# Prologue of a two-layer transformer kernel: split rests in a buffer of their own, the key sums on GpSimd behind the splits, the bias add between the first two quads

## The reference

```python
qkv = x @ W_attn + b_attn                     # 16 heads of 8 numbers each
q, k, v = heads(qkv)
s = einsum('bhtd,bhsd->bhts', q, k)
s = s - s.mean(axis=-1, keepdims=True)        # over all 1024 keys, later ones too
mad = abs(s).mean(axis=-1, keepdims=True) + 1e-06
s = s / mad * score_gain
s = where(causal, s, -1000.0)
r = maximum(s, 0.0) ** 4
att = r / (r.sum(axis=-1, keepdims=True) + 1e-06)
y = (att @ v) @ W_proj + b_proj
x = layernorm(x + y)
```

## Time and profile before

| what | value |
|---|---|
| median of the runs | 1172.78 us (1169.59, 1172.78, 1176.74) |
| the profiled execution, its own time | 1178.61 us |
| its span | 1176.9 us |
| TensorE, VectorE, ScalarE, GpSimd busy | 84%, 63%, 47%, 30% of the span |
| mean granted TensorE clock | 0.875 of full speed |
| prologue, to the first score matmul | 43.3 us |
| end of the first attention's quads | about 390 us |

### The profile page before, as it was taken

One profiled execution on the slowest core, in us unless ns is written; L12 is line 12 of the kernel. 1 busy time (PEld: TensorE's weight loads), 2 busy tenths in 40 slices (PEclk: granted clock), 3 DMA queues, 4 the chain that ended last, 5 costly groups with the idle time before them and its releaser, 6 DMA issues.

```text
span 1176.9 us, 18267 instructions
## 1 busy us (share of the span) xinstructions
PE 987.0 (84%) x6011; PEld 479.5 (41%) x6011; DVE 746.4 (63%) x1543; ACT 556.4 (47%) x607; POOL 351.6 (30%) x785
## 2 busy tenths in 40 slices
PE   5699999999999675398745788999999887999996
PEld 3222222223222543387742433333333226566664
DVE  5778788787887566443224895777877305644446
ACT  2578778777777321222213304555555773222222
POOL 3043343443344400267751202333333440000000
PEclk8599799998988778599986556999999997999998
DMA  4401101101100302056522422221121100000001
GB/s 129 143 1 41 41 1 40 40 1 39 40 1 1 122 9 67 15 137 151 142 25 63 170 83 82 83 64 62 47 77 42 43 1 28 14 14 27 13 13 36
DMA packets 45655, 63.27 MB, mean 54 GB/s; under 512 B 7720, under 2 KB 33672, under 8 KB 42120
## 3 DMA queue, kind: packets, MB, share of 16 engines
q1 hardware_dynamic: 39968, 58.11, 15.8%
q0 software_dynamic: 5632, 4.46, 2.6%
HBM read 50.69 MB, written 11.86 MB: 53 GB/s over the span
## 4 chain that ended last, share of the span: by engine, by line
PE 53%; DVE 21%; issue 10%; POOL 6%; ACT 5%; DMA 4%; DVEq 0%; SPq 0%; POOLq 0%; ACTq 0%
PE acc_ps L748 10%; PE causal_ps L1135 9%; DVE mx L498 6%; PE acc_ps L1042 6%; PE tail_ps L988 5%; PE tail_ps L1145 5%; PE causal_ps L1025 3%; DVE R L1424 3%; PE causal_ps L710 3%; POOL moe_rows L1983 2%; DMA moe_rows<-out_e,idx_out 2%; DVE tails L1430 2%; PE causal_ps L721 2%; ACT EX L1312 2%; POOL G L1967 2%
## 5 line engine op out<-in xcount | busy, mean ns | idle before, releaser
L1312 ACT ACTIVATE EX<-causal_ps 128x1024 f32<-128x1024 f32 (+1 forms) x160 | 146.8, 938 | 157.0 <-PE causal_ps L1025 155.9
L498 DVE TENSOR_REDUCE mx<-tail_ps 128x1 f32<-128x512 f32 x266 | 157.6, 632 | 41.2 <-PE tail_ps L991 22.7
L1205 ACT ACTIVATE R<-R 128x2048 f32<-128x2048 f32 (+1 forms) x80 | 135.3, 1731 | 2.0 <-DVE R L1424 1.9
L1135 PE MATMUL causal_ps<-XT,w 128*128 128x512 f32 x256 | 117.4, 606 | 2.6 <-DVE hid_f L1802 1.9
L1424 DVE TENSOR_SCALAR R<-causal_ps 128x1024 f32<-128x1024 f32 (+1 forms) x96 | 102.5, 1082 | 17.2 <-PE causal_ps L710 16.7
L988 PE MATMUL tail_ps<-KM,QM 72*128 72x512 bf16 (+1 forms) x320 | 105.1, 357 | 8.7 <-DVE mx L498 3.0
L1025 PE MATMUL causal_ps<-QE,KE 75*128 75x512 bf16 (+3 forms) x384 | 102.6, 338 | 8.5 <-ACT EX L1312 3.1
L1430 DVE TENSOR_REDUCE tails<-causal_ps 128x1 f32<-128x768 f32 (+5 forms) x88 | 89.6, 1019 | 25.4 <-PE causal_ps L721 24.8
L1348 ACT ACTIVATE act_f<-causal_ps 128x512 f32<-128x512 f32 x64 | 38.2, 597 | 130.1 <-PE causal_ps L1135 130.1
L1212 ACT ACTIVATE R<-R 128x1792 f32<-128x1792 f32 (+4 forms) x80 | 96.9, 1263 | 0.0
L748 PE MATMUL acc_ps<-R,sum_sel 128*32 128x512 f32 (+3 forms) x768 | 88.2, 534 | 6.6 <-ACT Ysb L1218 6.6
(11 more groups left out here) (266 smaller groups left out, 1604.9 us busy)
## 6 DMA issues: line engine op xcount, KB each, us to landing
QS<-q_parts SPq DMA_DIRECT2D x8, 576.0 KB
KS<-k_parts SPq DMA_DIRECT2D x24, 192.0 KB
QM<-q_parts SPq DMA_DIRECT2D x8, 576.0 KB
KM<-k_parts SPq DMA_DIRECT2D x24, 192.0 KB
QE<-q_parts SPq DMA_DIRECT2D x8, 576.0 KB
KE<-k_parts SPq DMA_DIRECT2D x24, 192.0 KB
wg<-in_wg_t SPq DMA_DIRECT2D x16, 256.0 KB
wu<-in_wu_t SPq DMA_DIRECT2D x16, 256.0 KB
```

What stands on the lines that cost most here:

```text
L498: return reduce(mx[:, par, hh, o0:o0 + step * (cnt - 1) + 1:step], scores[:, 0:cnt * w].rearrange("p (c w) -> p c w", w=w), AX.X, op, **how)
L1135: mm = pe.matmul(banks[2 * ring + o], w[:, k, m * P:(m + 1) * P], XT[:, n * BANK:(n + 1) * BANK], start=True, stop=True)
L1205: act.activation(R4[:, rp, h0:h0 + 2, 0:width], R1[:, rp, h0:h0 + 2, 0:width], ACT.Square).then_inc(squared, 1)
L1312: act.activation(EX[:, rp, hh, 0:width], causal_ps[hh % 2][:, 0:width], ACT.Exp, scale=float(D) ** -0.5).then_inc(exp_done, 1)
```

## The change

`proj` moves to the second half of R4 and the rests get the first half of R4, `rests0`. So q and k stay whole while the splits go on, and VectorE no longer waits for the key-sum matmuls. On VectorE the block sums L1401 now come behind the splits and the copy of v; the table `later` and the operations L1403, L1405 and L1406 are gone from it. GpSimd gets them, as a chain: one copy and six additions of 128x1 from the last block backward, and the spread over the heads. TensorE makes the key-sum matmuls of both batches at the end of the prologue, ahead of the first score matmul. ScalarE waits for them before its first quad, since it writes R4 there. VectorE copies `corr` out inside the first quad, at the start of step 1. It no longer waits for the last ScalarE copies before its first relu. GpSimd adds the bias to X behind its share of quad 0.

```diff
@@ tensors @@
-        later = sb("later", [P, KT - 1, KT], F32, A)
-        k_later = sb("k_later", [P, KT - 1, KT], F32, A)
-        k_after = sb("k_after", [P, KT - 1], F32, A)
+        k_after = sb("k_after", [P, B, KT - 1], F32, A)
...
-        proj = R1[:, :, :, :].rearrange("p a h t -> p (a h t)").rearrange("p (m t) -> p m t", t=T)
+        proj, rests0 = R4[:, 1, :, :], R4[:, 0, :, :]
@@ tensor engine: behind the loop over the projections, no longer in it @@
-                    pe.wait_ge(corr_ready, b + 1)
-                    for i in range(KT - 1):
-                        mm = pe.matmul(acc_ps[:, b * BANK + i * H:b * BANK + (i + 1) * H],
-                                       proj[:, 2 * b, i * P:(i + 1) * P], k_heads[:, b, i, :], start=True, stop=True)
-                    mm.then_inc(corr_full, 1)
+            for b in range(B):
+                pe.wait_ge(corr_ready, b + 1)
+                for i in range(KT - 1):
+                    mm = pe.matmul(acc_ps[:, b * BANK + i * H:b * BANK + (i + 1) * H],
+                                   proj[:, 2 * b, i * P:(i + 1) * P], k_heads[:, b, i, :], start=True, stop=True)
+                mm.then_inc(corr_full, 1)
@@ scalar engine @@
-            cut_parts(0, proj)
+            cut_parts(0, proj, rests0)
...
             act.wait_ge(part_done, 2 * REP * B)
+            act.wait_ge(corr_full, B)
             quad(0, 0, first=True)
@@ vector engine, in the loop over b @@
-                dve.wait_ge(rest_done, 2 * REP * b + 2)
-                link(dve.tensor_reduce(k_tiles[:, b, :], k.rearrange("p (i t) -> p i t", t=P), AX.X, ALU.add))
-                dve.wait_ge(upto_ready, 6)
-                link(dve.tensor_tensor(k_later[:, :, :], later[:, :, :],
-                                       k_tiles[:, b, :].unsqueeze(1).broadcast_to([P, KT - 1, KT]), ALU.mult))
-                link(dve.tensor_reduce(k_after[:, :], k_later[:, :, :], AX.X, ALU.add))
-                dve.tensor_tensor(k_heads[:, b, :, :], k_after[:, :].unsqueeze(2).broadcast_to([P, KT - 1, H]),
-                                  own_head[:, :].unsqueeze(1).broadcast_to([P, KT - 1, H]), ALU.mult
-                                  ).then_inc(corr_ready, 1)
-                dve.wait_ge(corr_full, b + 1)
-                take_rests(0, b, proj)
+                take_rests(0, b, rests0, proj)
                 dve.wait_ge(v_full, b + 1)
...
+                dve.tensor_reduce(k_tiles[:, b, :], k.rearrange("p (i t) -> p i t", t=P), AX.X, ALU.add
+                                  ).then_inc(key_sums, 1)
-            for b in range(B):
-                ins = dve.tensor_copy(corr[...], acc_ps[...])
-            ins.then_inc(corr_full, 1)
-            dve.wait_ge(part_done, 2 * REP * B)
+            def take_corr():
+                dve.wait_ge(corr_full, B)
+                for b in range(B):
+                    ins = dve.tensor_copy(corr[...], acc_ps[...])
+                ins.then_inc(corr_full, 1)
...
+                    if j == STEP_AT[1] and first:
+                        take_corr()
@@ gpsimd @@
+            def sum_later_keys(b):
+                pool.wait_ge(key_sums, b + 1)
+                pool.tensor_copy(k_after[:, b, KT - 2:KT - 1], k_tiles[:, b, KT - 1:KT]).then_inc(key_step, 1)
+                for i in range(KT - 3, -1, -1):
+                    pool.wait_ge(key_step, (KT - 1) * b + KT - 2 - i)
+                    pool.tensor_tensor(k_after[:, b, i:i + 1], k_after[:, b, i + 1:i + 2], k_tiles[:, b, i + 1:i + 2], ALU.add
+                                       ).then_inc(key_step, 1)
+                pool.wait_ge(key_step, (KT - 1) * (b + 1))
+                pool.tensor_tensor(k_heads[:, b, :, :], k_after[:, b, :].unsqueeze(2).broadcast_to([P, KT - 1, H]),
+                                   own_head[:, :].unsqueeze(1).broadcast_to([P, KT - 1, H]), ALU.mult
+                                   ).then_inc(corr_ready, 1)
+
+            pool.wait_ge(upto_ready, 4)
+            sum_later_keys(0)
+            pool.wait_ge(v_sb, 1)
+            take_v(0, 0)
+            sum_later_keys(1)
+            pool.wait_ge(v_sb, B)
+            quad(0, 0, after=0)
             pool.wait_ge(x_in, 16)
             pool.wait_ge(w_in, 16 * 2)
             pool.tensor_tensor(X[:, :, :], X[:, :, :], YT[:, 0, 0:P].unsqueeze(1).broadcast_to([P, NT, P]),
                                ALU.add).then_inc(res_in, 1)
-            pool.wait_ge(upto_ready, 2)
-            pool.wait_ge(v_sb, 1)
-            take_v(0, 0)
-            pool.wait_ge(v_sb, B)
-            quad(0, 0, after=0)
             quad(1, 1, after=1)
```

More of the change, by code:

```diff
@@ L290, in build @@
         own_done = sem("own_done")
+        key_sums = sem("key_sums")
+        key_step = sem("key_step")
         A.close()
@@ L1169, in rests, with cut_parts @@
                 return 2 * REP * b + 2 * n + m + 1 if layer == 0 else 2 * REP * B + 2 * (REP - 1) * b + 2 * (n - 1) + m + 1
-            def cut_parts(layer, values):
+            def cut_parts(layer, values, rest_of):
                 for b in range(B):
@@ L1181, in cut_parts @@
                             at_least(act, part_out[m][n], 16 * (B * layer + b))
-                            src = causal_ps[m][:, :] if layer and n == 0 else values[:, 2 * b + m, :]
+                            src = (causal_ps[m][:, :] if layer and n == 0 else
+                                   (rest_of if n else values)[:, 2 * b + m, :])
                             act.activation(pt[:, m, n, :], src, ACT.Copy).then_inc(part_done, 1)
-            cut_parts(0, proj)
+            cut_parts(0, proj, rests0)
             def keep(g, par, s):
@@ L1303, in _ @@
                 act.activation(latent[:, n * BANK:(n + 1) * BANK], banks[n][0:2 * DC, :], ACT.Copy).then_inc(lat_sb, 1)
-            cut_parts(1, projE)
+            cut_parts(1, projE, projE)
             def exps_of(g, par, s, hh):
@@ L1385, in take_rests @@
                         dve.wait_ge(part_done, 2 * REP * (B * layer + b) + 2 * n + m + 1)
-                        dve.tensor_tensor(rest, values[m][:, :] if values and n == 0 else rest, pt[:, m, n, :],
+                        src = (values[m][:, :] if layer else values[:, 2 * b + m, :]) if n == 0 else rest
+                        dve.tensor_tensor(rest, src, pt[:, m, n, :],
                                           ALU.subtract).then_inc(rest_done, 1)
@@ L1864, in _ @@
                         ).then_inc(upto_ready, 1)
-            pool.memset(later[:, :, :], 1.0).then_inc(upto_ready, 1)
             pool.memset(own_head[:, :], 0.0).then_inc(upto_ready, 1)
-            pool.wait_ge(upto_ready, 4)
-            pool.affine_select(out=later[:, :, :], in_=later[:, :, :], compare_op=ALU.is_gt, fill=0.0, base=0,
-                               pattern=[[-1, KT - 1], [1, KT]], channel_multiplier=0).then_inc(upto_ready, 1)
+            pool.wait_ge(upto_ready, 3)
             for d in range(D):
```

5 lines of the change are left out of this document (3 added, 2 removed).

## The result

| | kernel before | changed kernel |
|---|---|---|
| median of all runs | 1173.14 us (11 runs) | 1165.29 us (11 runs) |
| ratio of times (95% interval) | 1 | 0.9927 (0.9897 to 0.9956) |
| the profiled execution, its own time | 1178.61 us | 1168.55 us |
| its span, mean granted clock | 1176.9 us, 0.875 | 1166.8 us, 0.883 |
| first score matmul | 43.30 us | 35.82 us |

The changed kernel is faster by 0.73%, 8.6 us (5.2 to 12.1). Executions more than 1.5% above the fastest of their kernel are left out of every ratio, here 1178.63 and 1184.72 us of the changed kernel's eleven.

A forecast was written before the change was run, and what follows sets the result against it. The prologue, one chain almost wholly on VectorE until the first score matmul, was taken as the bound. Terms -8.0 + 1.6 + 0.45, about -6.0 us on the median 1172.8, gave 1166.8 us, range 1161.0 to 1172.0.

The forecast's parts named there:

- Batch 0, -8.0: Prologue, batch 0: 9.25 us leave VectorE's chain, 1.25 us for the block sums stay: -8.0 us.
- Batch 1, +1.6: Prologue, batch 1: 5.29 us leave, but block sums, GpSimd chain and key-sum matmuls now precede the first scores: +1.6 us.
- The copies, +0.45: Quad 0, step 0 to 1: VectorE's copies of `corr`, free before, cost +0.45 us.
- The add to X, 0: Between GpSimd's quads 0 and 1: the 4.49 us add fits into 5.66 us of idle time and costs 0.
- The lock on batch 1's mean removal and subtractions: Prologue: VectorE could stand for GpSimd's batch 0 work, at most 0.40 us, left out of the sum.
- The cover by the stack: End of prologue: the stack's load lands at 30.2, 6.7 us before the first score matmul at 36.9.
- Rival 1: Start of quad 0: the clock rises early and stays, 2 us more gained, at most 3: 1164.3 us; chance 0.15.
- Rival 2: Boundaries between quads: clock dips of 3.9 us each change in number; one fewer, chance 0.10; one or two more, 0.12.
- dips as many as before: Between quads: main case, the sum as worked out with an unchanged number of clock dips, 1165.3 to 1168.5 us; chance 0.50.

The follow-up runs named there:

- c_after: The changed kernel, unaltered, run again beside the kernel before; ratio 0.9911 against the kernel before.
- e7: The changed kernel with a second, unused add of the same size behind the add to X; ratio 0.9901 against the kernel before.
- e1: The kernel before with only GpSimd's add to X moved behind its share of quad 0; ratio 0.9962 against the kernel before.
- e2: The changed kernel with the add to X put back in the prologue, ahead of GpSimd's key sums; ratio 0.9936 against the kernel before.
- e4: The changed kernel with batch 1's key-sum matmuls moved behind the fourth score job of quad 0; ratio 0.9896 against the kernel before.
- e11: The kernel of e4 run once more; ratio 0.9874 against the kernel before.
- e5: The changed kernel with 22 unused TensorE matmuls between the key-sum matmuls of batch 0 and batch 1; ratio 0.9956 against the kernel before.
- e8: The changed kernel with two unused GpSimd adds ahead of batch 1's key sums, delaying the first score matmul to 43.00; ratio 0.9954 against the kernel before.
- e3: The changed kernel with batch 1's key sums back on VectorE, behind the block sums; ratio 0.9943 against the kernel before.
- late-matmul kernels: e4 and e11, the changed kernel with batch 1's key-sum matmuls moved into quad 0; ratios 0.9896 and 0.9874 against the kernel before.
- e6: The kernel before with only the new buffer for q, k and the rests, and the waits it asks for; ratio 0.9936 against the kernel before.

## Why the prediction was right, and where it was off

- **The mechanism and the forecast.** -6.0 us was forecast, -6.4 on the first score matmul and +0.45 on the `corr` copies. From the mean removal of batch 0 the first score matmul comes after 23.49 us in both executions of the change, and after 30.70 before: -7.2, with the 0.36 us of the copies -6.9. It was forecast at 36.9 and came at 35.82 and, in c_after, at 36.95; that the second hits is luck, since everything in that execution was 1.1 us late. The measured time moved by 8.6 (5.2 to 12.1) and 10.5 (6.2 to 14.8): above the forecast, within the range.
- **Batch 0, -8.0.** q of batch 1 starts 8.44 us earlier, 0.27 of it because q of batch 0 did. Measured -8.2.
- **Batch 1, +1.6.** From q of batch 1 to the first score matmul it was 43.30 - 28.40 = 14.90 us, and is 35.82 - 19.96 = 15.86, in c_after 36.95 - 21.08 = 15.87. Measured +1.0. Half of the 0.6 us between them is the GpSimd chain, taken at 2.6, which is 2.28 (30.49 to 32.77); another 0.2 is the step from the key-sum matmuls to the scores. Its steps are 0.27 apart, where I had taken 0.34 from chained selects: those were 0.214 us long each and these are 0.19. By spacing it was still nearer than by spans (1.5), as the Trainium skill (Perfetto Trace Analysis, GPSIMD Engine Instruction) has it. Between the matmuls and the scores there is no handover: the scores start 3.01 us after the start of the key-sum matmuls, where 3.17 + 0.05 was taken.
- **The copies, +0.45.** On the chain for 0.36 us.
- **The add to X, 0.** It fits with 1.15 us to spare, forecast 1.2; e7 shows that even a mask more than 3 us late does not reach the end of quad 1. Its price in the old place was 4.0 us at `k_heads` (e1), and 3.7 us in the changed kernel (e2).
- **The lock on batch 1's mean removal and subtractions** (kept in the range at up to 0.40 us, by the Trainium skill, SBUF — State Buffer, Who interferes with whom): GpSimd's key sums of batch 0 were done when the mean removal of batch 1 began at 22.72, and the copy of v, 22.41 to 22.81, met only its first 0.1 us; it took its usual 0.75 us. Here the price was nothing; e2 shows that the same two engines can cost each other 3.7 us at this instruction.
- **The cover by the stack, 6.7 us before it would bind.** The changed kernel's first score matmul was not released by the stack; e4 and e11 uncovered it and measured 6.0 and 6.2 us from the start of the last issue to landing, where 5.86 was taken from layer 2.
- **Rival 1, the early clock.** In the profile of the change the clock rose at 53 and stayed (0.99 from 53 to 60) and the first eviction came 9.0 us earlier, 1.5 more than the first score matmul. In c_after it was 0.50 from 53 to 60 and the first eviction came 4.9 us earlier, 1.4 less. So in these two executions it is neither a gain nor a loss of the change but a draw, and e5 shows that the first 13 us hardly gain by it.
- **Rival 2, the dips.** They spread the times, as expected, by about 4 us at a time, but only a part of them lies between quads. The six distances together are 252.6 us in the profile before, 255.1 in that of the change and 244.1 in c_after; the stretch from the last eviction to the end is 789.1, 787.6 and 794.9. So the profiled execution of the change had no fewer dips between quads than that of the kernel before, and c_after lost behind the quads most of what it saved in them. I took their number as the same in both kernels. The step that did not hold is that sentence, "dips as many as before": over all executions the change has a mean clock of 0.886, the kernel before 0.880. Of the 0.006, 0.0023 is the shorter stretch at the low clock; the rest is 0.0036, by the line 2.8 us. The mean time is 10.8 us lower, 6.9 of it the prologue with the copies; this 2.8 fits most of what is left, as an argument from the line and not as a measurement of the dips.

**What stays open** is why the clock is higher. The time at which the quads start does not explain it, since e8 starts them where the kernel before does and has 0.8826, and e3 has 0.8808 with the earliest start but the late-matmul kernels. Nor does the move of the add, since e1 has 0.8810. With 11 to 12 runs each and a spread of 4 us, chance is not excluded for e3, e6 and e8. No run puts q, k and the rests back into the first half of R1 with the rest of the change in place.

## What to carry over

A GpSimd operation beside a VectorE chain is priced by the VectorE instruction that stands for it: look for one much longer than its twin elsewhere, and see whether a GpSimd operation ends just before it does. A buffer that undoes a wait moves the bound to what stood in line behind the awaited work on its engine, here TensorE's projections, so the order of that engine has to move with it. Where executions differ by the granted clock, compare kernels at one clock before reading small differences, and read the shift itself from the milestones of the profile, counted from a point that the executions share: four executions of the changed prologue differ by up to 1.45 us at the first score matmul, and by nothing from the mean removal to it. Two parts of a change tried alone need not add up to it; where they don't, compare them stage by stage.

## What the runs showed of the hardware that I had not expected

- An instruction with a single SBUF input stood for GpSimd too: the mean removal, 4.43 us in place of 0.75 (e2), while a relu out of PSUM beside the same add in the changed kernel kept its 1.21 us (the row at 82.54), and block sums beside it 1.22 (e6, at 14.46).
- The same 14 records of key-sum matmuls took 1.74 us at 2.4 GHz (batch 0 in the profile of the change, granted 1.00 over 22.5 to 24.3) and 3.17 us at 1.2 GHz (batch 1, 0.50 over 32.8 to 35.8).
- Mean clock and time are tied at 7.8 us per 0.01 over 85 executions of one kernel (correlation -0.93): most of the spread from 1166.8 to 1186.5 us goes with TensorE's clock.
- The load of the stack takes 6.0 to 6.2 us from the start of its last issue with the stores of the other batch beside it, hardly more than the 5.86 us in layer 2.
